# Tail of a vision tower's token stage: row 5 ahead of the class token's value sums, the last window's chain ahead of tiles, column sums 6 and 7 on TensorE, four product buffers for GpSimd

## The chip, the cores and the metric

The kernel runs on one core of a Trainium2 chip. The metric is the device time of one execution in microseconds (us), median of the runs. The engines are called as the profile calls them: PE (TensorE's matmuls, PEld its weight loads), DVE (VectorE), ACT (ScalarE), POOL (GpSimd) and SP (which only starts DMAs here). Each works through its own queue in order and waits on semaphores.

## The reference, cut to what matters

128 samples go through a token stage (patches to nine window tokens and one class token), an attention layer over the ten tokens, a mixture of experts, a second attention layer and a low-rank mixture. The change lies where the first two meet. For one sample:

```python
# token stage, class token: attention of one query over the nine window tokens' values
gattn = softmax(einsum('bhd,bhnd->bhn', gq * scale, gk))
gagg = einsum('bhn,bhnd->bhd', gattn, gv)
cls_out = cls + gagg @ ga_proj_w + ga_proj_b
patch_out = local_out @ mod_w + mod_b
h = concatenate([patch_out, cls_out], axis=1)        # 10 tokens of 256 channels
# first attention layer, 16 heads of 16 channels; tokens are the sequence
x = layernorm(h)
q, k, v = x @ Wq.T + bq, x @ Wk.T + bk, x @ Wv.T + bv
scores = einsum('bhqd,bhkd->bhqk', q, k) * scale      # two of its corners are masked
out = einsum('bhqk,bhkd->bhqd', softmax(scores), v)
```

All data is float32.

## The kernel before, in words

The 128 samples lie on the 128 partitions; a tile is one token: 128 samples by 256 channels. `T = 10` tiles, 0 to 8 from the nine windows (`NW = 9`), 9 the class token (index `NW` in the code).

**Windows.** A window's chain after its local attention is: `aggregate` (DVE adds the weighted values), `turn_agg` (PE transposes), `copy_aggT` (ACT), `project_agg` (PE), `add_local` and `local_stats` (DVE), `turn_local` (PE), `copy_localT` (ACT), `project_mod` (PE), `local_std` (POOL), `copy_gv` (ACT), `token_out` (DVE, writes the tile of `h`). The chains of windows 7 and 8 (`NW - 2`, `NW - 1`) run in the tail.

**Class token.** `class_scores`, `lower_scores`, `exponent` and `weigh` make its nine weights; POOL multiplies the values by them (`value_prod`, 2304 elements) and folds the upper part onto the lower (`fold_values`, 1024); DVE adds up the remaining five slices (`aggregate(dve, NW, half)`, two instructions that write `agg`); then `turn_agg(pe, NW)`, `copy_aggT`, a projection with `w_gproj`, and DVE writes `h` (L1064), its statistics and `veps`. POOL raises the variance to the power -1/2 (`inverse_std`, L336, writes `rstd`), DVE makes `nmr` from `mv` and `rstd` (`shift_of`, L341), and only then can ACT normalize tile 9 (`norm_x`, L364).

**Attention's first half, tile by tile.** `norm_x` (ACT), `turn_x` (PE), `copy_xT` (ACT), `qk_tile` (PE, 512 columns: query and key) and `v_tile` (PE, 256 columns), `copy_qkv` (ACT). `qk_tile` of tile t writes bank 2 + t % 3, and waits until the row product of tile t - 3, which reads the query out of that bank, is done (`wait_qk_bank`).

**Scores.** PE doesn't multiply queries and keys here, since each sample has its own. For each tile t there are a row job (query t with keys 0 to t, (t + 1) * 256 elements) and a column job (key t with queries 0 to t - 1, t * 256 elements), each a product and then a sum over 16 channels into `a_s`. Row products and sums are DVE's (`row_scores`, L1365 and L1356), except row 6. Column products and row 6's are POOL's (`pool_scores`, L1121); their sums are DVE's (`pool_sums`, `add_up`, L1356), except those in `SUMS_ON_PE`: for columns 7, 8 and 9 PE adds by 16 matmuls with the identity into banks 0, 6 and 7 (`pe_sum_scores`, L1215) and ACT copies the result out (`copy_sums`, L1221). POOL's products go alternately into two buffers, `s_slot[1]` and `s_slot[2]`, parts of `w_raw`; a product waits until the one two jobs earlier has been summed.

Here "column 8" is the column job of tile 8, "row 6" the row job of tile 6.

**Order.** The tail is written out by hand, one list for each engine: `pe_end`, `act_end`, `pool_end`, `dve_end`. After them stands `phase`, a barrier of all five engines (L282), and then the softmax over all scores (`dve_attention`, whose first instructions are the two MEMSETs L1392 and L1393).

Of the kernel before, what the change touches and what calls it, by code (L numbers as in the profile page):

```python
# [25 lines left out]
NW = 9  # L26
# [6 lines left out]
T = NW + 1  # L33
# [30 lines left out]
def vision_tower(nc, d, out):  # L64
    ctx = ExitStack()
    with ctx:
# [861 lines left out]
        def pe_end(pe):  # L928
            pe.wait_ge(sem("summed"), NJ)
            pe_start_attention(pe, 0)  # L930
            turn_agg(pe, NW - 2)
            turn_x(pe, 0, 1)
            qk_tile(pe, 0, 0)
            project_agg(pe, NW - 2)
            v_tile(pe, 0, 0)
            turn_x(pe, 0, 2)
            qk_tile(pe, 0, 1)
            turn_local(pe, NW - 2)
            v_tile(pe, 0, 1)
            turn_x(pe, 0, 3)  # L940
            qk_tile(pe, 0, 2)
            project_mod(pe, NW - 2)
            v_tile(pe, 0, 2)
            turn_x(pe, 0, 4)
            qk_tile(pe, 0, 3)
            turn_agg(pe, NW - 1)
            v_tile(pe, 0, 3)
            project_agg(pe, NW - 1)
            turn_x(pe, 0, 5)
            qk_tile(pe, 0, 4)  # L950
            turn_local(pe, NW - 1)
            v_tile(pe, 0, 4)
            turn_x(pe, 0, 6)
            project_mod(pe, NW - 1)
            qk_tile(pe, 0, 5)
            v_tile(pe, 0, 5)
            turn_x(pe, 0, 7)
            qk_tile(pe, 0, 6)
            v_tile(pe, 0, 6)
            turn_x(pe, 0, 8)  # L960
            qk_tile(pe, 0, 7)
            v_tile(pe, 0, 7)
            qk_tile(pe, 0, 8)
            v_tile(pe, 0, 8)
            turn_agg(pe, NW)
            pe.wait_ge(sem("aggT_copied"), NW + 1)
            pe.wait_ge(sem("patch_made"), NW)
            mm_rows(pe, bank(7), aggT, w_gproj, 0, C).then_inc(sem("proj_done"), 1)
            turn_x(pe, 0, 9)
            qk_tile(pe, 0, 9)  # L970
            v_tile(pe, 0, 9)
            for t, kind in SUMS_ON_PE:
                pe_sum_scores(pe, t, kind)

        def act_end(act):
            copy_xT(act, 0, 0)
            copy_aggT(act, NW - 2)
            copy_xT(act, 0, 1)
            norm_x(act, 0, 2)
            exponent(act, NW - 1)  # L980
            copy_qkv(act, 0, 0)
            copy_xT(act, 0, 2)
            norm_x(act, 0, 3)
            copy_localT(act, NW - 2)
            copy_qkv(act, 0, 1)
            copy_xT(act, 0, 3)
            norm_x(act, 0, 4)
            copy_gv(act, NW - 2)
            copy_qkv(act, 0, 2)
            copy_xT(act, 0, 4)  # L990
            norm_x(act, 0, 5)
            copy_aggT(act, NW - 1)
            copy_qkv(act, 0, 3)
            copy_xT(act, 0, 5)
            norm_x(act, 0, 6)
            copy_localT(act, NW - 1)
            copy_qkv(act, 0, 4)
            copy_gv(act, NW - 1)
            copy_xT(act, 0, 6)
            normalized_scales(act, "attention 0", 1)  # L1000
            norm_x(act, 0, 7)
            exponent(act, NW)
            copy_qkv(act, 0, 5)
            copy_xT(act, 0, 7)
            normalized_scales(act, "attention 0", 2)
            norm_x(act, 0, 8)
            copy_qkv(act, 0, 6)
            copy_xT(act, 0, 8)
            copy_qkv(act, 0, 7)
            copy_qkv(act, 0, 8)  # L1010
            copy_aggT(act, NW)
            normalized_scales(act, "attention 0", 3)
            norm_x(act, 0, 9)
            copy_xT(act, 0, 9)
            copy_qkv(act, 0, 9)
            copy_sums(act)

        def pool_end(pool):
            value_prod(pool, NW - 1)
            local_std(pool, NW - 2)  # L1020
            fold_values(pool, NW - 1)
            pool_scores(pool, 0, 1, 3)
            inverse_std(pool, *batch_of("attention 0", 1))
            pool_scores(pool, 0, 3, 4)
            local_std(pool, NW - 1)
            pool_scores(pool, 0, 4, 5)
            inverse_std(pool, *batch_of("attention 0", 2))
            value_prod(pool, NW)
            fold_values(pool, NW)
            pool_scores(pool, 0, 5, 7)  # L1030
            inverse_std(pool, *batch_of("attention 0", 3))
            pool_scores(pool, 0, 7, T)

        def dve_end(dve, link):
            weigh(dve, link, NW - 1)
            add_local(dve, NW - 2)
            local_stats(dve, NW - 2)
            row_scores(dve, link, 0, 0)
            row_scores(dve, link, 0, 1)
            for half in range(2):  # L1040
                aggregate(dve, NW - 1, half)
            token_out(dve, NW - 2)
            add_eps(dve, "attention 0", 1)
            row_scores(dve, link, 0, 2)
            pool_sums(dve, link, 0, 1)
            add_local(dve, NW - 1)
            local_stats(dve, NW - 1)
            shift_of(dve, *batch_of("attention 0", 1))
            row_scores(dve, link, 0, 3)
            pool_sums(dve, link, 0, 2)  # L1050
            token_out(dve, NW - 1)
            add_eps(dve, "attention 0", 2)
            class_scores(dve, link)
            lower_scores(dve, link, NW)
            pool_sums(dve, link, 0, 3)
            weigh(dve, link, NW)
            shift_of(dve, *batch_of("attention 0", 2))
            row_scores(dve, link, 0, 4)
            pool_sums(dve, link, 0, 4)
            for half in range(2):  # L1060
                aggregate(dve, NW, half)
            row_scores(dve, link, 0, 5)
            dve.wait_ge(sem("proj_done"), NW + 1)
            dve.tensor_tensor(h_at(NW), bank(7), rows[:, 2 * C:3 * C], ALU.add).then_inc(sem("patch_made"), 1)  # L1064
            dve.wait_ge(sem("patch_made"), NW + 1)
            tile_stats(dve, "attention 0", NW, h_at(NW))
            add_eps(dve, "attention 0", 3)
            pool_sums(dve, link, 0, 5)
            row_scores(dve, link, 0, 6)
            pool_sums(dve, link, 0, 6)  # L1070
            shift_of(dve, *batch_of("attention 0", 3))
            for t in range(7, T):
                row_scores(dve, link, 0, t)
                pool_sums(dve, link, 0, t)
# [9 lines left out]
        HALF = T // 2  # L1084
# [14 lines left out]
            return jobs  # L1099


        SUMS_ON_PE = {(T - 3, "column"): 0, (T - 2, "column"): 6, (T - 1, "column"): 7}

        def summed_on_pe(layer, t, kind):
            return layer == 0 and (t, kind) in SUMS_ON_PE
# [61 lines left out]
        def wait_value_slot(eng, layer, t):  # L1167
# [3 lines left out]
            if i >= 2:  # L1171
                eng.wait_ge(sem("a_o_turned"), seen(layer, "o_turned", mine[i - 2] + 1))

        def pool_scores(pool, layer, first, last):

            jobs = pool_jobs(layer)
            for i, (t, kind, n) in enumerate(jobs):
                if first <= t < last:
                    pool.wait_ge(sem("a_qkv_made"), seen(layer, "qkv_made", 2 * t + 1))
                    if i >= 2 and summed_on_pe(layer, *jobs[i - 2][:2]):  # L1180
                        pool.wait_ge(sem("a_summed"), list(SUMS_ON_PE).index(jobs[i - 2][:2]) + 1)
                    elif i >= 2:
                        pool.wait_ge(sem("a_pool_prod_used"), used_count(layer, i - 2))
                    score_products(pool, kind, t, n, s_slot[1 + i % 2]).then_inc(sem("a_pool_prod_made"), 1)

        def pool_attention(pool, layer):
            if layer == 0:
                pool_route_constants(pool)
            else:
                inverse_std(pool, *batch_of("attention 1", 0))  # L1190
                inverse_std(pool, *batch_of("attention 1", 1))
                pool_scores(pool, layer, 0, 3)
                inverse_std(pool, *batch_of("attention 1", 2))
                pool_scores(pool, layer, 3, T)
            for t in VALUES_ON_POOL:
                pool.wait_ge(sem("a_p_made"), seen(layer, "p_made", 1 + t // HALF))
                wait_value_slot(pool, layer, t)
# [8 lines left out]
        def pe_sum_scores(pe, t, kind):  # L1206

            b = SUMS_ON_PE[t, kind]
            i = pool_jobs(0).index((t, kind, t))
            n, slot = t, s_slot[1 + i % 2]  # L1210
            pe.wait_ge(sem("a_pool_prod_made"), i + 1)
            pe.wait_ge(sem("patch_made"), NW + 1)
            by_channel = slot[:, 0:n * C].rearrange("p (x d) -> p x d", d=D16)
# [157 lines left out]
        def pool_sums(dve, link, layer, t):  # L1371

            before = len(pool_jobs(0)) * layer
            for i, (at, kind, n) in enumerate(pool_jobs(layer)):
                if at == t and not summed_on_pe(layer, at, kind):
                    dve.wait_ge(sem("a_pool_prod_made"), before + i + 1)
                    add_up(dve, kind, at, n, s_slot[1 + i % 2]).then_inc(sem("a_pool_prod_used"), 1)
                    dve.wait_ge(sem("a_pool_prod_used"), used_count(layer, i))
                    clip(dve, link, layer, kind, at, n)

# [800 lines left out]
```

## Time and profile before

| | us |
|---|---|
| median of 3 runs (lowest, highest) | 887.18 (886.36, 888.2) |
| the profiled execution | 887.02 |
| its span, first to last instruction | 885.3 |
| busy PE, DVE, ACT, POOL in the span | 749.5, 548.3, 358.4, 396.1 |
| mean granted TensorE clock | 0.917 |

1.7 us lie around the span. The profile's page gives the busy shares over the whole program; the tail of the token stage is a stretch of some 50 us in it (about 390 to 442.5 us from the span's start), which is read from the timelines of the engines, one after another. In a timeline a row is a group of like instructions in sequence: start, duration, engine, line, operation, output<-input, shapes, count, and in brackets how long the engine stood idle before it and what ended that.

### The profile page before, as it was taken

What the parts mean: (1) busy time and instruction counts of PE and PEld (TensorE: products, weight loads), DVE (VectorE), ACT (ScalarE), POOL (GpSimd) and SP (SyncE); (2) the same over time, 40 slices, a digit from 0 to 9 for tenths busy, and PEclk for the clock granted to TensorE, in tenths of its full rate; (3) what the DMA queues carried; (4) which work ended last, traced back from release to release, by engine and by line L of the source; (5) the groups of instructions that cost most, each with busy time, mean ns of one, the idle gap of its engine ahead of it and who ended that gap; (6) DMA issues with size and microseconds to landing.
All of it is one profiled execution on the core that took longest, in us unless ns stands there. A gap on an engine that the chain in (4) does not pass through costs nothing.

```text
span 885.3 us, 13257 instructions
## 1 busy us (share of the span) xinstructions
PE 749.5 (85%) x4479; PEld 646.4 (73%) x4479; DVE 548.3 (62%) x1256; ACT 358.4 (40%) x897; POOL 396.1 (45%) x269
## 2 busy tenths in 40 slices
PE   2979999999999999984935964999999999580867
PEld 2869998898988986532835963999999998350756
DVE  1677877787777777667399643222222224799956
ACT  2465665665665655421000141444444443351131
POOL 4555757747757623575254302333333322144310
PEclk9899999999999999985968965999999998695899
DMA  8432132222221110000020038699998860400001
GB/s 269 143 123 80 47 91 77 79 82 83 83 83 42 39 58 1 1 0 0 1 96 1 25 129 324 245 325 325 339 326 332 322 241 19 147 1 0 1 1 60
DMA packets 34490, 102.77 MB, mean 116 GB/s; under 512 B 3624, under 2 KB 12152, under 8 KB 27000
## 3 DMA queue, kind: packets, MB, share of 16 engines
q1 hardware_dynamic: 31832, 94.84, 31.0%
q0 software_dynamic: 2592, 7.10, 2.1%
q8 instruction: 37, 0.61, 0.3%
q14 instruction: 29, 0.24, 0.1%
HBM read 95.75 MB, written 6.17 MB: 115 GB/s over the span
## 4 chain that ended last, share of the span: by engine, by line
PE 72%; DVE 19%; POOL 3%; DMA 2%; issue 1%; ACT 1%; SPq 1%; POOLq 0%; DVEq 0%; ACTq 0%
PE banks L1533 11%; PE banks L1541 11%; PE banks L287 9%; PE banks L289 9%; PE banks L288 9%; PE banks L294 6%; PE banks L1241 5%; PE banks L300 4%; DVE a_o L1418 3%; DVE a_prod L1149 3%; PE banks L1215 2%; DVE a_s L1356 2%; PE banks L1275 2%; PE banks L1871 1%; DVE w_raw L1365 1%
## 5 line engine op out<-in xcount | busy, mean ns | idle before, releaser
L401 POOL TENSOR_TENSOR x_lo<-xraw,x_hi 128x640 fp32r<-128x640 f32 x81 | 129.4, 1605 | 109.8 <-ACT x_hi L395 109.8
L287 PE MATMUL banks<-wc_hi,x_hi 128*128 128x256 f32 x405 | 121.8, 301 | 18.0 <-POOL x_lo L401 12.7
L1631 ACT ACTIVATE hid<-banks,b 128x128 f32<-128x128 f32 x216 | 79.3, 367 | 109.6 <-PE banks L1533 109.5
L288 PE MATMUL banks<-wc_lo,x_hi 128*128 128x256 f32 x405 | 116.4, 287 | 0.0
L289 PE MATMUL banks<-wc_hi,x_lo 128*128 128x256 f32 x405 | 116.4, 287 | 0.0
L287 PEld LDWEIGHTS banks<-wc_hi,x_hi 128*128 128x128 f32 x405 | 79.5, 196 | 20.5 <-issue 12.9
L1790 DVE TENSOR_TENSOR res<-banks,xb 128x256 f32<-128x256 f32 x27 | 11.5, 425 | 126.9 <-PE banks L1541 126.9
L288 PEld LDWEIGHTS banks<-wc_lo,x_hi 128*128 128x128 f32 x405 | 79.6, 196 | 1.8 <-issue 0.2
L289 PEld LDWEIGHTS banks<-wc_hi,x_lo 128*128 128x128 f32 x405 | 79.2, 195 | 0.0
L1275 PE MATMUL banks<-ident,a_prod 128*128 128x128 f32 x372 | 50.6, 301 | 32.7 <-POOL a_prod L1149 32.7
L424 DVE BATCH_NORM_STATS2 stats<-banks 128x6 f32<-128x256 f32 x81 | 34.6, 427 | 69.6 <-ACT pe_sb L418 68.9
L418 ACT ACTIVATE pe_sb<-banks 128x256 f32<-128x256 f32 x81 | 31.0, 383 | 111.8 <-PE banks L289 111.8
L1275 PEld LDWEIGHTS banks<-ident,a_prod 128*128 128x128 f32 x372 | 50.4, 218 | 34.4 <-POOL a_prod L1149 19.5
L287 PE MATMUL banks<-wkv_hi,xg_hi 128*128 128x512 f32 x162 | 70.9, 438 | 4.4 <-DVE xg_lo L485 4.2
L1533 PEld LDWEIGHTS banks<-xT,w_raw 128*128 128x128 f32 x448 | 67.5, 195 | 5.7 <-ACT xT L1619 0.9
L1533 PE MATMUL banks<-xT,w_raw 128*128 128x128 f32 x448 | 69.3, 279 | 0.5 <-ACT xT L1619 0.5
L1241 PE MATMUL banks<-a_w,a_xT 128*128 128x512 f32 (+1 forms) x160 | 65.9, 550 | 1.9 <-DVE w_raw L1365 1.8
L1669 POOL TENSOR_TENSOR y<-bve,mhalf 128x1 f32<-128x1 f32 x27 | 20.4, 755 | 104.6 <-DVE bve L1798 104.6
L1121 POOL TENSOR_TENSOR w_raw<-a_qkv 128x512 f32<-128x512 f32 (+9 forms) x15 | 47.2, 3151 | 44.6 <-ACT a_qkv L1312 20.7
L1541 PE MATMUL banks<-w_raw,hid 128*128 128x256 f32 x224 | 66.9, 380 | 0.0
L336 POOL TENSOR_TENSOR rstd<-veps,mhalf 128x5 f32<-128x5 f32 (+5 forms) x31 | 35.2, 1136 | 67.7 <-DVE veps L354 50.9
L1533 PEld LDWEIGHTS banks<-xT,w1more 128*128 128x128 f32 x416 | 61.8, 191 | 4.7
(293 smaller groups left out, 1830.0 us busy)
## 6 DMA issues: line engine op xcount, KB each, us to landing
w_raw<-in_w SPq DMA_DIRECT2D x28, 1024.0 KB
xraw<-in_x_main SPq DMA_DIRECT2D x27, 768.0 KB
w1more<-in_w SPq DMA_DIRECT2D x13, 1024.0 KB
w2more<-in_w SPq DMA_DIRECT2D x13, 1024.0 KB
xraw<-in_x_rest SPq DMA_DIRECT2D x27, 114.0 KB
yl<-y_rows SPq DMA_DIRECT2D x2, 1028.0 KB, 7.0
a_w<-in_qkv_w SPq DMA_DIRECT2D x2, 768.0 KB, 5.2
x_rows<-w_raw SPq DMA_DIRECT2D x5, 256.0 KB, 2.0
```

Of the source, the lines that this page charges most:

```text
L287: pe.matmul(dst, a[0], b[0], start=start, stop=False)
L288: pe.matmul(dst, a[0], b[1], start=False, stop=False)
L289: return pe.matmul(dst, a[1], b[0], start=False, stop=stop)
L294: last = pe.matmul(dst, aT[:, c * P:(c + 1) * P], w[:, c, a:b], start=(c == 0), stop=(c == CH - 1))
L300: last = pe.transpose(dst[:, c * P:(c + 1) * P], src[:, c * P:(c + 1) * P], ident[:, :])
L401: pool.tensor_tensor(x_lo[:, i % RING_X, :], xraw[:, k].rearrange("p c b -> p (c b)"), x_hi[:, i % RING_X, :], ALU.subtract).then_inc(sem( ...
L1121: return eng.tensor_tensor(slot[:, 0:n * C].rearrange("p (s c) -> p s c", s=n), a_qkv[:, 0:n, first:first + C], a_qkv[:, t, second:second ...
L1241: last = pe.matmul(dst, a_xT[:, t % 2, c * P:(c + 1) * P], a_w[layer][:, c, a:b], start=(layer == 1 and c == 0), stop=(c == CH - 1))
L1275: last = pe.matmul(bank(t % 2, c * P, (c + 1) * P), value_slot(t)[:, k * C + c * P:k * C + (c + 1) * P], ident[:, :], start=(k == 0), stop ...
L1533: last = pe.matmul(bank(fc % 2, 0, P), weights_of(s)[0][:, c * FF + fc * P:c * FF + (fc + 1) * P], xT[:, s % 2, c * P:(c + 1) * P], start= ...
L1541: last = pe.matmul(down_bank(s), hid[:, s % 2, fc, :], weights_of(s)[1][:, fc * C:(fc + 1) * C], start=(fc == 0), stop=(fc == FC - 1))
L1631: act.activation(hid[:, s % 2, fc, :], bank(fc % 2, 0, P), ACT.Gelu, bias=b1[:, bass.ds(e * FC + fc, 1)]).then_inc(sem("gelu_made"), 1)
```

## The change

Four things are changed, all in the tail of the token stage:

1. In `dve_end` row 5's product and sum stand ahead of the class token's two `aggregate` instructions, no longer behind them; column 5's sum goes ahead of the class token's output, and `shift_of` of batch 3 (tile 9) stands ahead of row 6's sum.
2. The chain of window 8 stands one to two steps earlier between the tiles in `pe_end` and `act_end`.
3. `SUMS_ON_PE` now holds columns 6 (bank 0) and 7 (bank 6). Columns 8 and 9 are summed by DVE.
4. POOL has four places for its products: the two parts of `w_raw` and two parts of `a_prod` (`job_place`, `job_slot`). Jobs are numbered 0 to 9: columns 1 to 5, row 6, columns 6 to 9. Their places are 0, 1, 0, 1, 2, 3, 0, 1, 2, 3. A product waits for the last earlier use of its place. `pool_scores` now takes job numbers, and column 6 stands behind `inverse_std` of batch 3. In the second attention layer order and buffers stay as they were.

```diff
+            turn_agg(pe, NW - 1)
             turn_x(pe, 0, 4)
             qk_tile(pe, 0, 3)
-            turn_agg(pe, NW - 1)
+            project_agg(pe, NW - 1)
             v_tile(pe, 0, 3)
-            project_agg(pe, NW - 1)
+            turn_local(pe, NW - 1)
             turn_x(pe, 0, 5)
+            project_mod(pe, NW - 1)
             qk_tile(pe, 0, 4)
...
             inverse_std(pool, *batch_of("attention 0", 2))
             value_prod(pool, NW)
             fold_values(pool, NW)
-            pool_scores(pool, 0, 5, 7)
+            pool_scores(pool, 0, 4, 6)
             inverse_std(pool, *batch_of("attention 0", 3))
-            pool_scores(pool, 0, 7, T)
+            pool_scores(pool, 0, 6, T)
...
+            row_scores(dve, link, 0, 5)
             for half in range(2):
                 aggregate(dve, NW, half)
-            row_scores(dve, link, 0, 5)
+            pool_sums(dve, link, 0, 5)
...
-            pool_sums(dve, link, 0, 5)
-            row_scores(dve, link, 0, 6)
+            shift_of(dve, *batch_of("attention 0", 3))
             pool_sums(dve, link, 0, 6)
-            shift_of(dve, *batch_of("attention 0", 3))
...
-        SUMS_ON_PE = {(T - 3, "column"): 0, (T - 2, "column"): 6, (T - 1, "column"): 7}
+        SUMS_ON_PE = {(T - 4, "column"): 0, (T - 3, "column"): 6}
...
+        def job_place(layer, i):
+
+            return i % 2 if layer == 1 or i < 4 else (2, 3, 0, 1)[i % 4]
+
+        def job_slot(layer, i):
+            k = job_place(layer, i)
+            return s_slot[1 + k] if k < 2 else a_prod[:, k - 2, :]
...
+            for i in range(first, last):
+                t, kind, n = jobs[i]
+                pool.wait_ge(sem("a_qkv_made"), seen(layer, "qkv_made", 2 * t + 1))
+                earlier_use = [j for j in range(i) if job_place(layer, j) == job_place(layer, i)]
+                if earlier_use:
+                    pool.wait_ge(sem("a_pool_prod_used"), used_count(layer, earlier_use[-1]))
+                score_products(pool, kind, t, n, job_slot(layer, i)).then_inc(sem("a_pool_prod_made"), 1)
```

POOL's queue before, from the class token's value product (L597) and fold (L604) to the last product of the tail; 1280 is column 5, the first 1792 row 6, 1536 column 6, and then columns 7, 8 and 9:

```order
L597 TENSOR_TENSOR vprod<-gv_sb,attn 128x2304
L604 TENSOR_TENSOR vprod<-vprod 128x1024
L1121 TENSOR_TENSOR w_raw<-a_qkv 128x1280
L1121 TENSOR_TENSOR w_raw<-a_qkv 128x1792
L1121 TENSOR_TENSOR w_raw<-a_qkv 128x1536
L336 TENSOR_TENSOR rstd<-veps,mhalf 128x1
L1121 TENSOR_TENSOR w_raw<-a_qkv 128x1792
L1121 TENSOR_TENSOR w_raw<-a_qkv 128x2048
L1121 TENSOR_TENSOR w_raw<-a_qkv 128x2304
```

And the same stretch of POOL's queue in the changed kernel:

```order
L597 TENSOR_TENSOR vprod<-gv_sb,attn 128x2304
L604 TENSOR_TENSOR vprod<-vprod 128x1024
L1120 TENSOR_TENSOR a_prod<-a_qkv 128x1280
L1120 TENSOR_TENSOR a_prod<-a_qkv 128x1792
L336 TENSOR_TENSOR rstd<-veps,mhalf 128x1
L1120 TENSOR_TENSOR w_raw<-a_qkv 128x1536
L1120 TENSOR_TENSOR w_raw<-a_qkv 128x1792
L1120 TENSOR_TENSOR a_prod<-a_qkv 128x2048
L1120 TENSOR_TENSOR a_prod<-a_qkv 128x2304
```

Column 6 moved behind `rstd`, and four of the six score products write `a_prod`.

DVE's queue before, from column 4's sum (4x16) through the class token's `agg` and output (L1064) to its `nmr`:

```order
L1356 TENSOR_REDUCE a_s<-w_raw 128x4x16
L614 TENSOR_REDUCE agg<-vprod 128x128 x2
L1365 TENSOR_TENSOR w_raw<-a_qkv,banks 128x1536
L1356 TENSOR_REDUCE a_s<-w_raw 128x96
L1064 TENSOR_TENSOR h<-banks,rows 128x256
L347 BN_STATS stats<-h 128x6
L349 BN_AGGR mv<-stats 128x2
L354 TENSOR_SCALAR veps<-mv 128x1
L1356 TENSOR_REDUCE a_s<-w_raw 128x5x16
L1356 TENSOR_REDUCE a_s<-w_raw 128x112
L1356 TENSOR_REDUCE a_s<-w_raw 128x6x16
L341 SCALAR_TENSOR_TENSOR nmr<-mv,rstd 128x1
```

The same place in the changed kernel, up to row 6's sum:

```order
L1362 TENSOR_REDUCE a_s<-w_raw 128x4x16
L1371 TENSOR_TENSOR w_raw<-a_qkv,banks 128x1536
L1362 TENSOR_REDUCE a_s<-w_raw 128x96
L614 TENSOR_REDUCE agg<-vprod 128x128 x2
L1362 TENSOR_REDUCE a_s<-a_prod 128x5x16
L1065 TENSOR_TENSOR h<-banks,rows 128x256
L347 BN_STATS stats<-h 128x6
L349 BN_AGGR mv<-stats 128x2
L354 TENSOR_SCALAR veps<-mv 128x1
L341 SCALAR_TENSOR_TENSOR nmr<-mv,rstd 128x1
L1362 TENSOR_REDUCE a_s<-a_prod 128x112
```

Row 5 (1536 and 96) stands ahead of `agg`, column 5's sum (5x16) ahead of the output, and nothing stands between `veps` and `nmr`.

DVE's last rows ahead of the softmax in the changed kernel; 8x16 and 9x16 are the two sums that it takes over:

```order
L1371 TENSOR_TENSOR w_raw<-a_qkv,banks 128x2304
L1362 TENSOR_REDUCE a_s<-w_raw 128x144
L1362 TENSOR_REDUCE a_s<-a_prod 128x8x16
L1371 TENSOR_TENSOR w_raw<-a_qkv,banks 128x2560
L1362 TENSOR_REDUCE a_s<-w_raw 128x160
L1362 TENSOR_REDUCE a_s<-a_prod 128x9x16
L1398 MEMSET a_s 128x16
```

On PE the three groups of 16 matmuls behind tile 9 (112, 128 and 144 columns wide) became two (96 and 112 wide).

## Rows read from the trace of the kernel before

**Rows 1.** Waits, 389 to 443 us: engine line waited for, total, times, longest.

```profile
DVE a_s L1392 <- ACTq L282: 14.2, 1, 14.2
```

**Rows 2.** Timeline of PE, 366 to 446 us: start us, us, then as explained.

```profile
385.88 0.49 PE L1239 MATMUL banks<-bias_r,pick 64*128 64x512 f32 x1
...
388.52 1.13 PE L1241 MATMUL banks<-a_w,a_xT 128*128 128x256 f32 x4
393.31 0.76 PE L1239 MATMUL banks<-bias_r,pick 64*128 64x512 f32 x1 [3.65 <-DVE w_raw L1365]
...
399.96 0.38 PE L300 MATMUL banks<-ident,agg 128*128 128x128 f32 x2
400.88 1.13 PE L294 MATMUL banks<-w_gproj,aggT 128*128 128x256 f32 x4 [0.53 <-ACT aggT L634]
413.50 0.69 PE L300 MATMUL banks<-ident,a_xn 128*128 128x128 f32 x2 [11.49 <-ACT a_xn L364]
...
420.90 21.10 PE L1215 MATMUL banks<-w_raw,ident 128*128 128x112 f32 x96
```

**Rows 3.** Timeline of ACT, 360 to 446 us: the first and last copied sum.

```profile
427.22 0.26 ACT L1221 ACTIVATE a_s<-banks 128x112 f32<-128x112 f32 x1 [5.74 <-PE banks L1215]
...
442.03 0.29 ACT L1221 ACTIVATE a_s<-banks 128x144 f32<-128x144 f32 x1 [7.55 <-PE banks L1215]
```

**Rows 4.** Timeline of DVE, 360 to 446 us.

```profile
383.91 2.74 DVE L1356 TENSOR_REDUCE a_s<-w_raw 128x80 f32<-128x1280 f32 x2
389.07 2.44 DVE L614 TENSOR_REDUCE agg<-vprod 128x128 f32<-128x640 f32 x2 [2.42 <-POOL vprod L604]
391.41 1.75 DVE L1365 TENSOR_TENSOR w_raw<-a_qkv,banks 128x1536 f32<-128x1536 f32 x1
...
402.11 0.42 DVE L1064 TENSOR_TENSOR h<-banks,rows 128x256 f32<-128x256 f32 x1 [7.16 <-PE banks L294]
...
403.32 3.53 DVE L1356 TENSOR_REDUCE a_s<-w_raw 128x80 f32<-128x1280 f32 x2
...
410.25 2.56 DVE L341 SCALAR_TENSOR_TENSOR nmr<-mv,rstd 128x1 f32<-128x1 f32 x1
412.74 2.27 DVE L1365 TENSOR_TENSOR w_raw<-a_qkv,banks 128x2048 f32<-128x2048 f32 x1
415.05 2.29 DVE L1356 TENSOR_REDUCE a_s<-w_raw 128x128 f32<-128x2048 f32 x1
...
419.95 2.55 DVE L1356 TENSOR_REDUCE a_s<-w_raw 128x144 f32<-128x2304 f32 x1
...
425.40 2.82 DVE L1356 TENSOR_REDUCE a_s<-w_raw 128x160 f32<-128x2560 f32 x1
```

**Rows 5.** Timeline of POOL, 360 to 446 us.

```profile
388.94 6.82 POOL L1121 TENSOR_TENSOR w_raw<-a_qkv 128x1280 f32<-128x1280 f32 x2
404.94 3.42 POOL L1121 TENSOR_TENSOR w_raw<-a_qkv 128x1536 f32<-128x1536 f32 x1 [9.18 <-DVE a_s L1356]
408.32 0.55 POOL L336 TENSOR_TENSOR rstd<-veps,mhalf 128x1 f32<-128x1 f32 x1
408.83 8.47 POOL L1121 TENSOR_TENSOR w_raw<-a_qkv 128x1792 f32<-128x1792 f32 x2
427.33 5.11 POOL L1121 TENSOR_TENSOR w_raw<-a_qkv 128x2304 f32<-128x2304 f32 x1 [10.03 <-PE banks L1215]
```

**Rows 6.** Timelines of POOL and of DVE, 44 to 52 us.

```profile
47.32 1.54 POOL L401 TENSOR_TENSOR x_lo<-xraw,x_hi 128x640 fp32r<-128x640 f32 x1
...
47.40 1.48 DVE L341 SCALAR_TENSOR_TENSOR nmr<-mv,rstd 128x5 f32<-128x5 f32 x1 [1.12 <-POOL rstd L336]
```

**Rows 7.** Windows, PE alone: stretch us, PE busy (x), granted clock, DMA share, GB/s.

```profile
366.00:389.60 23.60, 23.60 (x79) 1.00 0.00 0
...
393.30:399.90 6.60, 6.59 (x10) 0.51 0.00 0
...
560.00:780.00 220.00, 207.90 (x1343) 0.95 0.73 262
```

More of the change, by code:

```diff
@@ L943, in pe_end @@
             v_tile(pe, 0, 2)
+            turn_agg(pe, NW - 1)
             turn_x(pe, 0, 4)
             qk_tile(pe, 0, 3)
-            turn_agg(pe, NW - 1)
+            project_agg(pe, NW - 1)
             v_tile(pe, 0, 3)
-            project_agg(pe, NW - 1)
+            turn_local(pe, NW - 1)
             turn_x(pe, 0, 5)
+            project_mod(pe, NW - 1)
             qk_tile(pe, 0, 4)
-            turn_local(pe, NW - 1)
             v_tile(pe, 0, 4)
             turn_x(pe, 0, 6)
-            project_mod(pe, NW - 1)
             qk_tile(pe, 0, 5)
@@ L988, in act_end @@
             copy_gv(act, NW - 2)
+            copy_aggT(act, NW - 1)
             copy_qkv(act, 0, 2)
@@ L991, in act_end @@
             norm_x(act, 0, 5)
-            copy_aggT(act, NW - 1)
+            copy_localT(act, NW - 1)
             copy_qkv(act, 0, 3)
@@ L995, in act_end @@
             norm_x(act, 0, 6)
-            copy_localT(act, NW - 1)
+            copy_gv(act, NW - 1)
             copy_qkv(act, 0, 4)
-            copy_gv(act, NW - 1)
             copy_xT(act, 0, 6)
@@ L1021, in pool_end @@
             fold_values(pool, NW - 1)
-            pool_scores(pool, 0, 1, 3)
+            pool_scores(pool, 0, 0, 2)
             inverse_std(pool, *batch_of("attention 0", 1))
+            pool_scores(pool, 0, 2, 3)
+            local_std(pool, NW - 1)
             pool_scores(pool, 0, 3, 4)
-            local_std(pool, NW - 1)
-            pool_scores(pool, 0, 4, 5)
             inverse_std(pool, *batch_of("attention 0", 2))
@@ L1172, in wait_value_slot @@
                 eng.wait_ge(sem("a_o_turned"), seen(layer, "o_turned", mine[i - 2] + 1))
+        def job_place(layer, i):
[3 more added lines that the diff above has]
+            return s_slot[1 + k] if k < 2 else a_prod[:, k - 2, :]
         def pool_scores(pool, layer, first, last):
             jobs = pool_jobs(layer)
[L1177 to L1184, printed above, removed]
+            for i in range(first, last):
[5 more added lines that the diff above has]
+                score_products(pool, kind, t, n, job_slot(layer, i)).then_inc(sem("a_pool_prod_made"), 1)
         def pool_attention(pool, layer):
@@ L1191, in pool_attention @@
                 inverse_std(pool, *batch_of("attention 1", 1))
-                pool_scores(pool, layer, 0, 3)
+                pool_scores(pool, layer, 0, 1)
                 inverse_std(pool, *batch_of("attention 1", 2))
-                pool_scores(pool, layer, 3, T)
+                pool_scores(pool, layer, 1, HALF)
             for t in VALUES_ON_POOL:
@@ L1209, in pe_sum_scores @@
             i = pool_jobs(0).index((t, kind, t))
-            n, slot = t, s_slot[1 + i % 2]
+            n, slot = t, job_slot(0, i)
             pe.wait_ge(sem("a_pool_prod_made"), i + 1)
@@ L1376, in pool_sums @@
                     dve.wait_ge(sem("a_pool_prod_made"), before + i + 1)
-                    add_up(dve, kind, at, n, s_slot[1 + i % 2]).then_inc(sem("a_pool_prod_used"), 1)
+                    add_up(dve, kind, at, n, job_slot(layer, i)).then_inc(sem("a_pool_prod_used"), 1)
                     dve.wait_ge(sem("a_pool_prod_used"), used_count(layer, i))
```

## The prediction

> **What bounds the kernel now.** The change touches only the tail of the token stage, so I read what ends that tail, and then the chain back from it. The list of waits [rows 1] shows DVE idle for 14.2 us at the barrier: of all engines it had been done long before, and ACT came last. ACT's last act is the copy of column 9's sum [rows 3], at 442.03 + 0.29 = 442.32 us; DVE's own last sum ended at 425.40 + 2.82 = 428.22 [rows 4]. So PE's column sums end the tail: 21.1 us in one piece [rows 2], started when tile 9's products were done. Tile 9 began at 413.50, after 11.49 us in which PE waited for `a_xn`, thus for `nmr` of the class token. What held `nmr`? Backwards along DVE and POOL [rows 4, 5]: it ended at 412.81; `rstd` was made only at 408.87, since POOL's queue held column 6 ahead of it, and column 6 waited 9.18 us for a buffer that DVE freed with column 5's sum; the class token's output came at 402.11, after a wait of 7.16 us for PE; PE began `turn_agg` at 399.96, behind tile 8; and tile 8 had waited 3.65 us for row 5's product, which stood behind `agg` on DVE. After that wait PE ran at the lower clock level: granted 0.51 in 393.3 to 399.9, against 1.00 ahead of it [rows 7], that is 1.2 instead of 2.4 GHz.
>
> So the bound is one chain, row 5 -> tile 8 -> class token -> rstd -> nmr -> tile 9 -> PE's sums -> barrier, and DVE has 14 us of slack at its end.
>
> **The change, part by part.** All is counted from the profiled execution's start of span; its time is 887.02, 0.16 below the median.
>
> *Row 5 ahead of `agg`.* DVE ends column 4's sum at 383.91 + 2.74 = 386.65 [rows 4] and then stood idle 2.42 us for POOL's fold. Row 5 takes that hole: product 1.75, sum the same, so it ends at 390.2, its product at 388.4. Tile 7 leaves PE at 388.52 + 1.13 = 389.65 [rows 2]; tile 8's bank is then free, and the wait of 3.65 us is gone. With it goes the rest that was ahead of the low clock, so tile 8 costs what tile 7 did, 389.65 - 385.88 = 3.77, not 399.96 - 393.31 = 6.65. `turn_agg` can start at 393.4: 3.66 + 2.88 = 6.55 us earlier. What is late next? `agg` itself: 390.2 + 2.44 = 392.65, 0.75 us ahead of PE. So `agg` comes later than before (391.51) and that costs nothing, by 0.75 us.
>
> *The last window's chain ahead of tiles.* PE, ACT and DVE do the same work in another order. It gives the class token's weights earlier (1 to 2 us by the rows of tiles 3 to 5), but by the above neither the fold nor `agg` decides: PE's tile 8 does. It only widens the 0.75 us. On the other side, `copy_qkv` of tiles 2 and 3 is now queued behind `copy_aggT` and `copy_localT` on ACT, and column 2, column 3 and the row products wait for that; and an earlier `lower_scores` can meet column 4's product on POOL. All of it has over 10 us to be made good before tile 8. I take 0, with -0.3 and +1 as ends.
>
> *Class token to `veps`.* As before: 402.11 - 399.96 = 2.15 to the output, and to the end of `veps` at 403.40 another 1.29 (the next row starts at 403.32, overlapping). So 393.4 + 3.45 = 396.85. DVE sums column 5 (1.49) in the hole between `agg` and the output: column 5's product is in its own place and done at about 391.8 (the first of the two in 6.82 us, 2.9) [rows 5]. Row 6's product ends at 395.8, one microsecond ahead of `veps`, so POOL is free.
>
> *Four places, and column 6 behind `rstd`.* `rstd` runs 396.9 to 397.45 with nothing ahead of it. In before it had 4.9 us from `veps` to its start. POOL then starts column 6 at once: its place (job 2's) is long free, and in before the next product started 0.51 us after `rstd` [rows 5], so 397.4 to 400.85. And here the trace has a warning. `nmr` is one element wide and took 2.56 us, 410.25 to 412.81, when the POOL product that started at 408.83 ran (1792 elements; two products in 8.47, so the first ends at about 412.8). At 47.32 the same happened from the very situation of the change [rows 6]: DVE waits for `rstd`, POOL's next instruction starts 0.08 us ahead of `nmr`, and `nmr` takes 1.48 us, to 48.88, where the POOL instruction ends (48.86). `nmr` reads two tensors in SBUF. I therefore let `nmr` end with column 6, at 400.9. Against 412.81 that is 11.9 us earlier; without the hold it would be 15.2.
>
> The Trainium skill says this of the port pair that DVE and GpSimd share (page "SBUF — State Buffer", section "Who interferes with whom"): a DVE instruction with two SBUF inputs contends with a GpSimd one that reads SBUF, and whichever issues first has it for its whole length. The trace agrees, with 2.56 and 1.48 us for an instruction of 0.15. By a reading without that rule the sum would be 3.3 us better.
>
> *PE's end.* From the end of `nmr` to `turn_x` of tile 9 0.7 us (412.81 to 413.50), from there to the first sum 7.4 (413.50 to 420.90) [rows 2]. PE rests from 395.5 to 401.6, which is more than the 3.65 us after which it came back at the low level, so I keep these 7.4 us as they are. Sums start at 409.0. Column 7 took 427.22 - 420.90 = 6.3 [rows 2, 3]; columns 8 and 9 together 14.8, 7.4 each at a mean width of 136 against 112, so 0.046 us a column of width; column 6 is 96 wide: 5.6. Both products are made by then (column 7's at 404.9). PE ends at 409.0 + 11.9 = 420.9, ACT's copy at 421.2.
>
> *DVE's end.* It takes over columns 8 and 9 and gives up column 6. From `nmr` at 400.9: row 6's sum, 2.0 (3.53 less column 5's 1.49); rows 7, 8, 9 as before, 428.22 - 412.74 = 15.5, all products with one operand in a PSUM bank, which ran at full speed beside POOL in before; column 8's sum 2.3 and column 9's 2.6, priced by the row sums of 2048 and 2304 elements (2.29, 2.55) [rows 4]. Together 22.4, with gaps 22.45: 423.35. POOL's products for them: columns 7, 8 and 9 take 4.0, 4.5 and 5.1 [rows 5] from 400.85, so 414.5 for the last; DVE wants it at 420.8. DVE, not PE, is now last, by 2.2 us, and 0.14 us later (442.46 - 442.32) the softmax starts: 423.5 against 442.46 before, 19.0 us earlier.
>
> *After the barrier* nothing is tied to a clock time: all engines and the expert weights' loads wait for the barrier or the softmax. In the second attention layer jobs keep order, places and waits. I take 0.
>
> 887.02 - 19.0 = 868.0; on the median's scale 868.1.
>
> **The rivals.**
>
> *A. `nmr` gets ahead of column 6.* Then DVE and PE both end 3.3 us earlier (423.35 - 3.3 = 420.0): 864.8. Against it stands the pair in [rows 6].
>
> *B. A margin of about 1 us breaks:* `agg` later than tile 8 (0.75), or row 6's product not done when `veps` and `rstd` come (1.0). Each microsecond missed costs one: 869 to 872. For it: both margins are small against my error over the tiles before.
>
> *C. PE's sums run at the lower level.* Tile 8 against tile 7 gives 6.65 / 3.77 = 1.76; the sums then take 20.9, PE ends at 430.2 and not DVE: 874.9. Against it: in before the sums, after the same 7.4 us of work, had the full level.
>
> *D. The change doesn't do the early part:* the class token is ready only when it was (`veps` at 403.40), because something that I don't see holds tile 8 or `turn_agg`. What is left is column 6 behind `rstd`, and the shorter sums: `rstd` 403.95, column 6 to 407.4, DVE 22.45 more, 429.85 + 0.14: 12.5 us won, 874.5.
>
> *E. Slower:* the chip grants PE less in the expert stage, because a rest of PE ahead of it is 19 us shorter. 560 to 780 us ran at a mean of 0.95 [rows 7]. At 0.86 it costs 220 x (0.95 / 0.86 - 1) = 23 us, 891; from 0.874 downwards the whole gain is gone. Against it: PE is busy for all of 366 to 389.6 at 1.00, so long work doesn't lower the level; only waits did.
>
> **How the numbers follow.** Forecast 0.70, A 0.07, B 0.13, C 0.04, D 0.04, E 0.02. A, the forecast and B lie in 864.2 to 872.0, with 0.6 below A for the spread of runs; that is 0.90, and it covers the ends of the second part. A measurement tells about 0.2%, 1.8 us, from no change; all but E and a remainder are beyond it on the fast side: faster 0.96, same 0.02, slower 0.02.
>
> **What would show it.** In the trace of the changed kernel: no wait of PE ahead of tile 8, and its clock at 1.00 there; `turn_agg` of the class token at about 393.4; `rstd` at 397; `nmr` over 3 us long, ending with column 6's product; tile 9's transpose at 401.6; PE's sums of some 12 us, ended at 421; DVE the last ahead of the barrier with column 9's sum, near 423.4; no wait of POOL for PE. The forecast is wrong if `nmr` takes 0.15 us (A), if PE waits for `agg` (B), if the sums take 20 us (C), or if the stretch behind the barrier changes its length by over a microsecond (E).

## The result, and the profile after

| | before | changed |
|---|---|---|
| median of 4 runs each, same chip (lowest, highest), us | 887.32 (886.36, 888.2) | 867.57 (866.69, 868.25) |
| profiled execution, us | 887.02 | 867.38 |
| its span, us | 885.3 | 865.7 |
| ratio of the times, 95% interval | | 0.9777 (0.976 to 0.9794) |

The change makes the kernel 19.75 us faster (887.32 - 867.57). Forecast were 19.0 us and a time of 868.1, and the range of 864.2 to 872.0 holds the measured one. The profiled spans differ by 19.6 us. To see where, the tail is measured from one landmark to another that both kernels have: from the output of token tile 7 on DVE (L684) to the first MEMSET behind the barrier.

| profiled executions | ahead of tile 7's output | tail | behind the barrier |
|---|---|---|---|
| before | 365.81 | 76.65 | 442.84 |
| changed | 366.69 | 58.02 | 440.99 |
| difference | +0.88 | -18.63 | -1.85 |

Timeline of DVE in the changed kernel, 366 to 446 us (columns as in the rows of before); it answers to [rows 4]:

```profile
366.69 0.42 DVE L684 TENSOR_TENSOR h<-banks,rows 128x256 f32<-128x256 f32 x1 [1.53 <-ACT gv_sb L680]
...
378.73 2.33 DVE L582 TENSOR_TENSOR sc<-sc,smax 128x72 f32<-128x72 f32 x1
...
388.81 1.75 DVE L1362 TENSOR_REDUCE a_s<-w_raw 128x96 f32<-128x1536 f32 x1
390.60 2.45 DVE L614 TENSOR_REDUCE agg<-vprod 128x128 f32<-128x640 f32 x2
...
396.78 0.42 DVE L1065 TENSOR_TENSOR h<-banks,rows 128x256 f32<-128x256 f32 x1 [2.35 <-PE banks L294]
...
398.74 3.37 DVE L341 SCALAR_TENSOR_TENSOR nmr<-mv,rstd 128x1 f32<-128x1 f32 x1 [0.66 <-POOL rstd L336]
...
413.88 2.29 DVE L1362 TENSOR_REDUCE a_s<-a_prod 128x128 f32<-128x2048 f32 x1
...
421.91 2.55 DVE L1362 TENSOR_REDUCE a_s<-a_prod 128x144 f32<-128x2304 f32 x1
424.71 0.07 DVE L1398 MEMSET a_s<- 128x16 f32 x1 [0.25 <-DVEq L282]
```

Row 5's sum stands directly ahead of `agg`, with no wait. `nmr` is one element wide and 3.37 us long. From there to the barrier DVE has no wait at all, and the MEMSET behind the barrier waits 0.25 us for DVE's own queue, where in before it waited 14.2 us for ACT [rows 1]: DVE is the last engine now.

Timeline of PE in the same stretch; it answers to [rows 2]:

```profile
391.02 0.49 PE L1245 MATMUL banks<-bias_r,pick 64*128 64x512 f32 x1
...
394.63 0.38 PE L300 MATMUL banks<-ident,agg 128*128 128x128 f32 x2
...
402.79 0.69 PE L300 MATMUL banks<-ident,a_xn 128*128 128x128 f32 x2 [6.11 <-ACT a_xn L364]
...
409.37 11.56 PE L1221 MATMUL banks<-w_raw,ident 128*128 128x96 f32 x64
```

Tile 8 begins at 391.02 with no wait, and `turn_agg` 3.6 us later. PE's sums are two, of 11.56 us together, and end at 420.9, 3.8 us ahead of the barrier. Timeline of POOL, which answers to [rows 5]:

```profile
389.30 6.84 POOL L1120 TENSOR_TENSOR a_prod<-a_qkv 128x1280 f32<-128x1280 f32 x2
398.15 0.55 POOL L336 TENSOR_TENSOR rstd<-veps,mhalf 128x1 f32<-128x1 f32 x1 [2.01 <-DVE veps L354]
398.66 7.37 POOL L1120 TENSOR_TENSOR w_raw<-a_qkv 128x1536 f32<-128x1536 f32 x2
405.99 9.60 POOL L1120 TENSOR_TENSOR a_prod<-a_qkv 128x2048 f32<-128x2048 f32 x2
```

The only wait is that of `rstd` for `veps`. The waits of 9.18 us for a buffer and of 10.03 us for PE are gone. Column 6's product starts at 398.66, and `nmr`, released by the same `rstd`, 0.08 us behind it.

### The profile page after: what moved, and what is told of

It reads as the page before. It is cut to its first block, busy times and chain, and to the rows that moved or that the text cites. A ratio compares the mean times of both kernels' runs of the same rounds, so it can differ in the third digit from the quotient of the medians.

```text
span 865.7 us, 13191 instructions
## 1 busy us (share of the span) xinstructions
PE 733.8 (85%) x4447; PEld 634.3 (73%) x4447; DVE 555.5 (64%) x1257; ACT 357.3 (41%) x896; POOL 396.3 (46%) x269
## 4 chain that ended last, share of the span: by engine, by line
PE 67%; DVE 22%; POOL 3%; issue 2%; DMA 2%; SPq 1%; ACT 1%; POOLq 1%; DVEq 0%; ACTq 0%
PE banks L1539 11%; PE banks L1547 11%; PE banks L287 10%; PE banks L289 9%; PE banks L288 9%; PE banks L294 6%; PE banks L300 4%; DVE a_s L1362 4%; DVE a_o L1424 3%; DVE a_prod L1148 3%; PE banks L1247 2%; DVE w_raw L1371 2%; PE banks L1281 2%; PE banks L1877 1%; DVE a_p L1416 1%
## 5 line engine op out<-in xcount | busy, mean ns | idle before, releaser
L289 PE MATMUL banks<-wkv_hi,xg_lo 128*128 128x512 f32 x162 | 64.5, 398 | 0.0
L288 PE MATMUL banks<-wkv_lo,xg_hi 128*128 128x512 f32 x162 | 63.9, 395 | 0.0
```

The lines of the kernel that those rows point to most:

```text
L288: pe.matmul(dst, a[0], b[1], start=False, stop=False)
L289: return pe.matmul(dst, a[1], b[0], start=False, stop=stop)
```

## The experiments

Every kernel is the changed one with one edit, unless said otherwise. All profiles agree on the tail to a few hundredths of a microsecond (58.02, 58.03, 58.03 in three of the changed kernel, 76.65 and 76.65 in two of before), so experiments are compared by the tail. "Ratio" is that of the whole time to before in the same batch, with its interval.

**1. Row 5 put back behind `agg`.**

```diff
-            row_scores(dve, link, 0, 5)
             for half in range(2):
                 aggregate(dve, NW, half)
+            row_scores(dve, link, 0, 5)
             pool_sums(dve, link, 0, 5)
```

> The changed kernel with row 5 put back behind the class token's two agg instructions; all else stays. Theory: tile 8 on PE waits again for row 5's product. By the changed kernel's rows the fold ends at 389.34 us, agg would end at 391.85, the product at 393.6, and tile 7 leaves PE at 391.0: a wait of 2.6 us. If PE keeps the high clock level over that wait, the whole chain and the barrier come 2.6 to 2.8 us later (870.3); if it falls to the low level as it did after 3.65 us in the kernel before, 2.9 us more (873.2). Rival: row 5's place is worth nothing, the gain is all from column 6's place and the shorter sums: within 0.5 us of 867.6.

Measured: tail 62.32 us, 4.30 more; 871.19 us, ratio 0.9843 (0.9818 to 0.9868). Timeline of PE, and its granted clock in two stretches (us, PE busy, clock, DMA share, GB/s):

```profile
393.35 0.47 PE L1245 MATMUL banks<-bias_r,pick 64*128 64x512 f32 x1 [2.58 <-DVE w_raw L1371]
398.62 0.38 PE L300 MATMUL banks<-ident,agg 128*128 128x128 f32 x2
```

```profile
390.00:393.30 3.30, 0.76 (x4) 1.00 0.00 0
393.30:398.60 5.30, 5.25 (x10) 0.68 0.00 0
```

The wait is there, and of the two cases of the expectation neither but something between: tile 8 started at the high level (0.47 us for the first matmul), lost it during the query and key products and had it back for `v_tile` (0.38 us for its first matmul, as in the changed kernel), 5.27 us instead of 3.6. The row's place is worth 2.6 us of wait and 1.7 of clock.

**2. The last window's chain put back between the tiles** (the first part of the diff above, undone on PE and ACT).

> The changed kernel with the last window's chain put back between the tiles where it stood before, on PE and ACT. Theory: PE's tile 8 decides when the class token's turn_agg starts, not the weights; turn_agg within 0.5 us, time within 0.5 us of 867.6. The fold would end about 0.5 us later at most, since lower_scores was held 2.1 us by column 4's product in the changed kernel and would not be. Rival: the earlier chain is what brings agg ahead of PE, and without it PE waits for agg: 1 to 2 us slower.

Measured: tail 57.48 us, 0.54 less; `turn_agg` 27.39 us behind tile 7's output instead of 27.94. So this part of the change costs half a microsecond instead of bringing one. One half of it is a wait of PE of 0.25 us for `localT`, which stands in the changed kernel's timeline and not in this one; where the other half goes was not traced. Beside that, `lower_scores`' subtraction takes 0.23 us here, not 2.33 as above, since it no longer meets column 4's product (two microseconds off the path). The whole time was 869.44 us, ratio 0.9817 (0.9798 to 0.9835), thus not shorter, and outside the 0.5 us around 867.6 of the expectation: what lies behind the barrier was 3.5 us longer than in the changed kernel's first profile. More on that below.

**3. PE sums columns 7, 8 and 9 again, DVE column 6; four places kept.**

```diff
-        SUMS_ON_PE = {(T - 4, "column"): 0, (T - 3, "column"): 6}
+        SUMS_ON_PE = {(T - 3, "column"): 0, (T - 2, "column"): 6, (T - 1, "column"): 7}
```

> The changed kernel with PE summing columns 7, 8 and 9 again, DVE column 6, with the four places kept. Theory: PE's sums are the last again. They start at 409.4 us and take 21.1 instead of 11.6, DVE ends at about 420.9; the barrier comes at 431 instead of 424.7: 6.2 us slower, 873.8. Rival: the sums' number does not matter as long as no product waits for a buffer: within 1 us of 867.6.

Measured: tail 64.15 us, 6.13 more; 876.86 us, ratio 0.9906 (0.988 to 0.9932). Timelines of PE and DVE:

```profile
414.57 14.99 PE L1221 MATMUL banks<-a_prod,ident 128*128 128x128 f32 x64
```

```profile
430.03 0.07 DVE L1398 MEMSET a_s<- 128x16 f32 x1 [9.50 <-ACTq L282]
```

PE is the last again, and DVE waits 9.5 us at the barrier. The theory holds in the tail; that the profiled span is 9.6 and not 6.1 us up belongs again to what lies behind, which was 4.3 us longer.

**4. POOL back to two buffers in turn, two sums on PE.**

```diff
-            return i % 2 if layer == 1 or i < 4 else (2, 3, 0, 1)[i % 4]
+            return i % 2
...
-                if earlier_use:
+                if earlier_use and summed_on_pe(layer, *jobs[earlier_use[-1]][:2]):
+                    pool.wait_ge(sem("a_summed"), list(SUMS_ON_PE).index(jobs[earlier_use[-1]][:2]) + 1)
+                elif earlier_use:
                     pool.wait_ge(sem("a_pool_prod_used"), used_count(layer, earlier_use[-1]))
```

> The changed kernel with POOL back to two buffers in turn, all else as changed. Column 8's product then waits until PE has summed column 6 out of the same buffer, column 9's until PE has summed column 7. Theory: by the changed kernel's rows PE's first sum ends at 414.8 us, so column 8's product comes at 419.4 instead of 410.5, while DVE wants it at 413.9: DVE stands 5.5 us. The stretch from the output of token tile 7 to the first instruction behind the barrier is 58.0 us in the changed kernel and becomes 63.5; time 5.5 us up. Rival: the four places only matter for PE's three sums, with two sums and two buffers nothing waits: within 0.5 us of 58.0.

Measured: tail 63.64 us, 5.62 more; 875.04 us, ratio 0.9847 (0.9821 to 0.9873). Timelines of DVE and POOL:

```profile
418.74 2.29 DVE L1364 TENSOR_REDUCE a_s<-w_raw 128x128 f32<-128x2048 f32 x1 [5.64 <-POOL w_raw L1120]
```

```profile
414.09 4.55 POOL L1120 TENSOR_TENSOR w_raw<-a_qkv 128x2048 f32<-128x2048 f32 x1 [6.68 <-PE banks L1223]
```

The buffers and PE's sums are one chain: column 8's product waits for PE, and DVE for the product.

**5. `nmr` ahead of column 6's product.**

```diff
             inverse_std(pool, *batch_of("attention 0", 3))
+            pool.wait_ge(sem("nmr_made"), batch_of("attention 0", 3)[0] + 1)
             pool_scores(pool, 0, 6, T)
```

> The changed kernel with one wait added: POOL starts column 6 only when the class token's nmr is made. Theory: nmr took 3.37 us since column 6's product, which started 0.08 us ahead of it, kept it from SBUF; it then takes 0.15 us, tile 9 starts 3.2 us earlier on PE, DVE's last sums end 3.2 us earlier, POOL's products still come in time: 864.4. Rival: nmr is slow for another reason (a one-element instruction behind a semaphore of POOL), then it stays at over 3 us, POOL only starts later, and the time is 867.6 or up to 3 us more.

Measured: tail 55.12 us, 2.90 less; 863.07 us, ratio 0.9741 (0.9722 to 0.976). Timelines of DVE, POOL and PE:

```profile
397.37 0.16 DVE L341 SCALAR_TENSOR_TENSOR nmr<-mv,rstd 128x1 f32<-128x1 f32 x1 [0.66 <-POOL rstd L336]
```

```profile
397.61 7.40 POOL L1121 TENSOR_TENSOR w_raw<-a_qkv 128x1536 f32<-128x1536 f32 x2 [0.27 <-DVE nmr L341]
```

```profile
398.22 0.44 PE L300 MATMUL banks<-ident,a_xn 128*128 128x128 f32 x2 [2.91 <-ACT a_xn L364]
```

`nmr` ends 3.22 us earlier and takes 0.16 us; the rival falls. Of the 3.22 us 0.3 are lost, because DVE, which is now earlier, waits 0.35 us for column 8's product (here as in experiment 8, whose row is shown there).

**6. A longer product behind `rstd`:** POOL's last four in the order column 8, 6, 7, 9.

```diff
-            return [(t, kind, n) for t in range(T) for kind, n, pooled in score_jobs(layer, t) if pooled]
+            jobs = [(t, kind, n) for t in range(T) for kind, n, pooled in score_jobs(layer, t) if pooled]
+            return jobs[:6] + [jobs[8], jobs[6], jobs[7], jobs[9]] if layer == 0 else jobs
```

> The changed kernel with POOL's products in the order column 8, 6, 7, 9 behind rstd instead of 6, 7, 8, 9. Theory: nmr is kept as long as the product that starts just ahead of it runs. Column 8's takes about 4.55 us against 3.4, so nmr takes 4.5 instead of 3.37 us, and the stretch to the barrier becomes 59.15 instead of 58.0. Rival: nmr waits a fixed time or for part of the product: it stays at 3.4 us, the stretch at 58.0.

Measured: tail 59.12 us, 1.10 more; 871.37 us, ratio 0.9807 (0.9775 to 0.984). Timeline of DVE:

```profile
397.47 4.44 DVE L341 SCALAR_TENSOR_TENSOR nmr<-mv,rstd 128x1 f32<-128x1 f32 x1 [0.66 <-POOL rstd L336]
```

`nmr` is held to the end of whichever product starts just ahead of it: 3.37 us by one of 1536 elements, 4.44 by one of 2048.

**7. Column 6's product back ahead of `rstd`, in its own place.**

```diff
-            pool_scores(pool, 0, 4, 6)
+            pool_scores(pool, 0, 4, 7)
             inverse_std(pool, *batch_of("attention 0", 3))
-            pool_scores(pool, 0, 6, T)
+            pool_scores(pool, 0, 7, T)
```

> The changed kernel with column 6's product put back ahead of rstd in POOL's queue, its own place kept. Theory: row 6's product ends at 396.1 us, column 6's then at 399.6, rstd 1.4 us later than in the changed kernel, and nmr is kept by column 7's product of 4.0 us instead of column 6's of 3.4: nmr ends 2.0 us later, the stretch to the barrier becomes 60.0 instead of 58.0. Rival: since column 6 no longer waits for a buffer, its place in the queue is worth nothing: 58.0.

Measured: tail 59.91 us, 1.89 more; 871.84 us, ratio 0.981 (0.9783 to 0.9837). `nmr` began 2.16 us behind `veps` instead of 0.82 and took 3.90 us, as long as column 7's product.

**8. The wait of 5 and the old chain of 2 together.**

> The changed kernel with both: POOL starts column 6 only when the class token's nmr is made, and the last window's chain back between the tiles where it stood before. Theory: the two edits are worth 2.90 and 0.54 us of the stretch from the output of token tile 7 to the barrier, and add up, since one moves turn_agg and the other what follows it: 54.6 instead of 58.0. Rival: with nmr early something else has no margin left, and only the first is seen: 55.1. The whole time is not told apart to 0.5 us, since the stretch behind the barrier differs by up to 3.5 us from profile to profile.

Measured: tail 54.58 us; 864.15 us, ratio 0.9744 (0.9715 to 0.9773). The two add up. DVE's timeline shows what is short now:

```profile
409.12 2.29 DVE L1363 TENSOR_REDUCE a_s<-a_prod 128x128 f32<-128x2048 f32 x1 [0.35 <-POOL a_prod L1121]
```

**9. The kernel of 8, and row 6 summed by PE ahead of tile 9.** `pe_sum_scores` and `copy_sums` take a row as well; ACT copies row 6's sum behind `a_xT` of tile 9; column 9's product waits for PE's sum of row 6.

```diff
-        SUMS_ON_PE = {(T - 4, "column"): 0, (T - 3, "column"): 6}
+        SUMS_ON_PE = {(T - 4, "row"): 0, (T - 4, "column"): 6, (T - 3, "column"): 7}
...
+            pe.wait_ge(sem("a_xT_made"), 9)
+            pe_sum_scores(pe, 6, "row")
             turn_x(pe, 0, 9)
```

> The kernel with both of these edits, and row 6 summed by PE in the hole between the class token's projection and tile 9, with columns 6 and 7 behind tile 9 as changed (banks 0, 6, 7). Theory: PE works from the projection through, so that tile 9 runs at the high clock level: the 6.1 us of row 6's sum delay tile 9 by 3.2 us, tile 9 gets 1.6 us shorter, and DVE, which is last, is rid of row 6's sum of 2.0 us; the stretch to the barrier becomes 52.5 instead of 54.6. Rival: PE becomes the last again, since its sums start 1.6 us later and tile 9's copy comes too late for DVE's row 9: 54.6 or more.

Measured: tail 54.63 us, not the 52.5 expected; 863.74 us, ratio 0.9739 (0.9711 to 0.9767). Timelines of PE and DVE:

```profile
394.38 6.35 PE L1230 MATMUL banks<-a_prod,ident 128*128 128x112 f32 x32 [0.69 <-POOL a_prod L1125]
400.55 0.40 PE L300 MATMUL banks<-ident,a_xn 128*128 128x128 f32 x2
...
401.84 1.98 PE L1259 MATMUL banks<-a_w,a_xT 128*128 128x512 f32 x4
```

```profile
408.03 2.29 DVE L1374 TENSOR_REDUCE a_s<-a_prod 128x128 f32<-128x2048 f32 x1 [2.44 <-POOL a_prod L1125]
```

PE did as expected: tile 9 ran at the high level (1.98 us for four matmuls, where the changed kernel has 3.49). But the theory had left POOL out. It makes columns 6, 7 and 8 one behind another from 396.0 on, and DVE, rid of row 6, stands 2.44 us for column 8. POOL's products hold DVE now; neither theory nor rival had named them. Whether column 8's sum behind row 9 would give it back was not tried.

Two more profiles of the changed kernel and one of before belong to the stretch behind the barrier:

> The changed kernel itself once more, for a second profile. From the barrier to the first expert's transposes it took 99.8 us where the kernel before took 103.1, with the same code. Theory: the difference is the moment at which the granted clock falls in the router's stretch, which is not tied to the code; a second execution can give anything from 99.8 to 103.1, and the stretch ahead of the barrier is the same 58.0 within 0.1. Rival: the change itself shortens it, and it is 99.8 again within 0.3.

> The changed kernel for a third profile: 58.0 us to the barrier; behind it 99.8 again within 0.3 if that length belongs to the kernel, anything up to 103.4 if it is chance.

> The kernel before once more, for a second profile. Theory: from the output of token tile 7 to the barrier 76.65 us within 0.1; behind it 103.1 us to the first expert's transposes if that length belongs to a kernel, anything from 99.8 to 103.4 if it is chance. The changed kernel gave 99.8 and 99.9 in two profiles, seven kernels with the same code there gave two values near 100.4 and five from 102.6 to 103.4.

Measured: changed kernel again, 868.01 us with a ratio of 0.9764 (0.9735 to 0.9793), tail 58.03; third profile, 869.13 us, tail 58.03; before again, 885.65 us, tail 76.65. From the barrier to the first expert's transposes: changed 99.81, 99.88, 100.58; before 103.09, 103.14. The other kernels fell into two groups: 100.33, 100.42, 100.30, 100.28 (experiments 1, 5, 8, 9) and 103.09, 102.55, 103.19, 103.32, 103.36 (2, 3, 4, 6, 7). The code there is the same in all. Granted clock in 8 us of it, 72 to 80 us behind the barrier, where PE makes the router's logits, in before and then in the changed kernel, once each:

```profile
514.46:522.46 8.00, 7.12 (x39) 0.59 0.26 98
```

```profile
496.71:504.71 8.00, 7.24 (x48) 0.70 0.22 82
```

In the slower group's experiment 2 it was 0.50 in the like stretch. PE falls to the low level there in every kernel, only sooner or later. The stretch holds a row of equal steps, each of two transposes and then four matmuls of 8 columns for the logits, and a step takes 0.62 us at the high level and 1.18 at the low one. The starts of two neighbouring steps in experiment 8 (100.30) and then of the same two in experiment 2 (103.09), rows of PE's timelines:

```profile
492.14 0.42 PE L300 MATMUL banks<-ident,w_raw 128*128 128x128 f32 x2
...
492.76 0.42 PE L300 MATMUL banks<-ident,w_raw 128*128 128x128 f32 x2
```

```profile
494.76 0.67 PE L300 MATMUL banks<-ident,w_raw 128*128 128x128 f32 x2
...
495.94 0.67 PE L300 MATMUL banks<-ident,w_raw 128*128 128x128 f32 x2
```

The last logits end 79.28 to 79.36 us behind the barrier in all seven profiles of the quicker group (the changed kernel's three among them) and 81.91 to 82.20 in the seven others. Nearly all that is left of the spread, such as 99.88 against 100.58 in two profiles of the changed kernel, is PE's wait for the DMA that fetches the first expert's rows (7.86 and 8.54 us). Of the changed kernel's repeats one missed the 0.3 us of its expectation by this, not by the clock.

That chance alone decides is unlikely, though not refuted: a kernel's repeats fell into the same group each time, with three and two profiles. The timed runs say the same of the experiments: their spans, less the tail of the kernel's profile, are on average 806.3 to 808.1 us for two sets of the changed kernel (its third profile is a single run, 809.4) and for experiments 1, 5, 8 and 9, and 809.8 to 811.5 for 2, 3, 4, 6 and 7, though the single runs of a set spread by about 2 to 7 us. Before lies between and across, with 807.8 to 809.7 in three sets. The chip isn't the cause: experiments 1 and 5 ran on the same one as 2 and 3. Nor is it the change as such, since experiments 2, 4, 6 and 7 keep most of it and have the 103, nor one part of it, since experiments 2 and 8 both lack the earlier chain and fall into different groups. What ties the moment to the kernel stays open.

## Why the prediction was right

*Row 5 ahead of `agg`, forecast 6.55 us on `turn_agg`.* From tile 7's output it came 34.15 us in before and 27.94 now: 6.21. Experiment 1 shows the mechanism. `agg` was ready 1.6 us ahead of PE (390.60 + 2.45 against 394.63), not 0.75; rival B had no part in it. The two moves that went with it, column 5's sum ahead of the output and `shift_of` ahead of row 6's sum, were not undone by themselves.

*The last window's chain, taken at 0 with ends at -0.3 and +1.* It costs 0.54 us. This is the difference between 6.55 and 6.21, and more: without it PE would have been 0.2 us better than forecast. The collision of `lower_scores` with column 4's product came as named (2.33 us), and was hidden as said.

*`veps` to `nmr`.* `rstd` was made at once; POOL had been idle 2.01 us. `nmr` ended with column 6's product. Forecast 11.9 us earlier than before, measured 47.00 - 35.42 = 11.58 from tile 7's output; the missing 0.3 is that of `turn_agg`. That rival A was worth 3.3 us is borne out by experiment 5 at `nmr` (3.22), but not at the barrier: 2.90 of it arrive there, since column 8's product then comes late for DVE, which the rival's sum had left out. Experiments 6 and 7 show that the hold is that of the product ahead, for three lengths of it (3.37, 3.90, 4.44 us).

*PE's end.* Column 6's and 7's sums took 11.56 us against 11.9. From tile 9's transpose to the first sum it was 6.58, not 7.4: the high level was back when tile 9's `v_tile` began (0.38 us for its first matmul), and in before only in the middle of it (0.58). This was mis-sized by 0.8 us and had no effect, since DVE is last; PE ended 3.8 us ahead of the barrier instead of 2.6.

*DVE's end.* From the end of `nmr` to that of column 9's sum 424.46 - 402.11 = 22.35 against 22.45. The sums out of `a_prod` cost what those out of `w_raw` had (2.29, 2.55). Tail: 18.63 us won against 19.0. (In rival C the 430.2 is the end of ACT's copy, 409.0 + 20.9 + 0.3, and not PE's; nothing hangs on it.)

*Four places and the two sums.* They were not priced by themselves. Experiments 3 and 4 give 6.13 and 5.62 us to each where the other is kept; experiment 7 gives 1.89 to column 6's place, experiment 1 4.30 to row 5's. These need not add up to 18.63, since each undoes a step of one chain while the others hide part of it; the four together were not undone in steps.

*Behind the barrier, taken at 0.* This is the step that was wrong, by a small amount: 1.85 us shorter in the first pair of profiles. In three and two profiles it is 440.99, 442.64, 442.64 against 442.84, 442.93, so 0.2 to 1.9. What the term left out is that the granted clock falls in the router's stretch at a moment that differs, though the code is the same. That stretch wins 2.5 to 3.3, and most of it is given back behind the experts: the first softmax product of the second attention layer (`a_p`) is still 2.5 us ahead (368.61 against 371.15 us behind the barrier in the second profiles), the first MEMSET of the last stage only 0.9 (412.76 against 413.68). That the whole comes out 0.5 us from the forecast is in part luck: in the profiled spans 1.85 us won behind the barrier stand against 0.3 lost in the tail and 0.88 lost ahead of tile 7's output, which the prediction didn't name. Rival E named the clock behind the barrier, but not the place: in the expert stage, the same 220 us from the barrier on (542.25 to 762.25), it is 0.96 against 0.95 in before. The prediction's remark there, that long work doesn't lower the level and only waits did, doesn't hold in the router's stretch: PE was busy for 7.24 of the 8 us in which its clock fell to a mean of 0.70.

Rivals C and D don't show: PE's sums ran at a granted 1.00, and the class token came early.

## What to carry to other kernels

When a chain hops from engine to engine, write down for each hop what is queued ahead of it on that engine: row 5's place (4.30 us) and column 6's (1.89 us) are both such moves of an instruction group out of the way of something that others wait for. An engine with 14 us of slack at the barrier can take work from the one that ends last, if the buffers of that work don't tie it back to the engine relieved. And where a small DVE instruction with two SBUF inputs is released by POOL, let POOL's next long instruction wait for it; that one wait brought 2.9 us here.

## What the runs showed of the hardware that was not expected

- The hold of `nmr` came with an order of 0.08 us: POOL's next instruction started 398.66, the DVE instruction released by POOL's previous one 398.74. It was so in all nine profiles of the changed queues without experiment 5's wait (three of the changed kernel, experiments 1, 2, 3, 4, 6 and 7), and it cost the whole of the product, 3.37, 3.90 or 4.44 us. What happens when DVE's starts first and POOL's runs into it no run shows; in experiment 5 POOL's next instruction starts only behind its end.
- After rests of 2.58 us (experiment 1) and 2.91 us (experiment 5) PE began at the high level, 0.47 us for the first matmul and 0.44 for the transposes, and lost it on the way; the clock of the whole tile was 0.68 in experiment 1. After rests of 3.65 us (before) and 6.11 us (changed) it began at the low one, 0.76 and 0.69 us for the same. The high level was back 5.3 us after tile 9 had begun in the changed kernel (402.79 to 408.09) and after about 6.5 in before.
- The same code behind the barrier takes 99.8 to 100.6 or 102.6 to 103.4 us, mainly by the moment at which the clock falls in a stretch of small matmuls. A kernel's tail can be forecast to 0.4 us and its time still be off by three.
